# Value products of two steps of four scores issued together in three groups of a turn

## What is computed

```python
...
    x = _L0_conv_ref(x, ...)   # group norm, attention over channels (32x32 per head), projection, + x
    x = _L1_conv_ref(x, ...)   # one head, 32 channels, softmax over 1024 positions, value of 128 channels
    x = _L2_conv_ref(x, ...)   # group norm, 8 heads of 32 channels, softmax over 1024 positions, projection, + x
    x = _L3_conv_ref(x, ...)   # the same with other weights, and the normed image added at the end
...
        sim = jnp.einsum('bhdi,bhdj->bhij', q, k)
        attn = jax.nn.softmax(sim, axis=-1)
        out = jnp.einsum('bhij,bhdj->bhid', attn, v)
```

## Time and profile before

| what | value |
|---|---|
| median of three runs | 3087.99 us |
| the profiled execution | 3084.11 us |
| its span, first to last instruction | 3082.3 us |
| mean granted TensorE clock | 0.963 |
| PE (TensorE matmul) busy | 2846.6 us, 92% |
| POOL (GpSimd) busy | 2179.4 us, 71% |
| DVE (VectorE) busy | 1858.1 us, 60% |
| ACT (ScalarE) busy | 1553.3 us, 50% |
| PE's share of the chain that ended last | 64% |

### The profile page before, as it was taken

How to read it: one execution, slowest core, us unless ns; L and a number is a source line. 1 busy time by engine, 2 the same in 40 slices (tenths; PEclk the granted TensorE clock), 3 DMA queues, 4 the chain that set the end, 5 groups by cost and what they waited for, 6 DMA issues and landing times.

```text
span 3082.3 us, 36214 instructions
## 1 busy us (share of the span) xinstructions
PE 2846.6 (92%) x13152; PEld 1405.6 (46%) x13152; DVE 1858.1 (60%) x3293; ACT 1553.3 (50%) x2794; POOL 2179.4 (71%) x746
## 2 busy tenths in 40 slices
PE   6688979999999999999999999999999999999998
PEld 4345434544445444554445544464444544444442
DVE  1264557557665667556675666756766576767663
ACT  1233435445564455545554555644555445555554
POOL 3225757677775877768776777867777587798877
PEclk8779989999999999999999999999999999999999
DMA  2240054133341234330343323503343123333340
GB/s 72 44 67 13 23 80 68 24 43 56 44 83 24 32 57 71 57 53 16 43 87 40 53 45 48 90 14 43 57 64 62 30 39 43 57 56 43 43 58 15
DMA packets 74388, 150.87 MB, mean 49 GB/s; under 512 B 9121, under 2 KB 10657, under 8 KB 74210
## 3 DMA queue, kind: packets, MB, share of 16 engines
q1 hardware_dynamic: 74210, 148.56, 31.9%
HBM read 20.46 MB, written 16.78 MB: 12 GB/s over the span
## 4 chain that ended last, share of the span: by engine, by line
PE 64%; DMA 12%; ACT 9%; DVE 8%; issue 3%; POOL 3%; SPq 2%; ACTq 0%; POOLq 0%; DVEq 0%
PE psum L1277 15%; PE psum L1302 11%; PE psum L1246 10%; DMA Q<-lo 7%; PE psum L1221 6%; PE psum L1190 5%; ACT prob L907 4%; PE psum L1198 4%; DVE maxpart L1030 3%; PE psum L1298 3%; DMA K<-hi 3%; PE psum L1123 2%; DMA Q<-max_rows 2%; DVE stats L939 2%; PE psum L1323 2%
## 5 line engine op out<-in xcount | busy, mean ns | idle before, releaser
L1030 DVE TENSOR_REDUCE maxpart<-psum 128x1 f32<-128x512 f32 x2176 | 1412.0, 684 | 816.5 <-PE psum L1246 793.0
L907 ACT ACTIVATE prob<-psum 128x512 f32<-128x512 f32 x2176 | 1226.3, 596 | 960.9 <-PE psum L1277 925.1
L803 POOL TENSOR_TENSOR acc<-acc,prob 128x2048 f32<-128x2048 f32 (+1 forms) x322 | 1151.9, 3577 | 178.8 <-ACT prob L907 150.4
L1277 PE MATMUL psum<-Q,K 104*128 104x512 f32 x2048 | 1081.1, 530 | 96.1 <-ACT prob L907 73.6
L1246 PE MATMUL psum<-K,Q 96*128 96x512 f32 x2048 | 837.9, 413 | 36.9 <-DMA K<-hi 20.5
L1277 PEld LDWEIGHTS psum<-Q,K 104*128 104x128 f32 x2048 | 391.3, 192 | 799.0 <-ACT prob L907 474.1
L1302 PE MATMUL psum<-prob,vT 128*32 128x512 f32 x4096 | 577.0, 623 | 0.0
L803 POOL TENSOR_TENSOR vT<-vT,prob 128x2048 f32<-128x2048 f32 x123 | 560.8, 4559 | 19.4 <-ACT prob L907 8.3
L1246 PEld LDWEIGHTS psum<-K,Q 96*128 96x128 f32 x2048 | 399.8, 195 | 188.9 <-issue 90.9
L803 POOL TENSOR_TENSOR acc<-prob 128x2048 f32<-128x2048 f32 (+1 forms) x58 | 212.0, 3655 | 385.8 <-PE psum L1323 210.2
L1302 PEld LDWEIGHTS psum<-prob,vT 128*32 128x32 f32 x4096 | 100.6, 110 | 200.8 <-ACT prob L907 114.3
(11 more groups left out here) (121 smaller groups left out, 2130.4 us busy)
## 6 DMA issues: line engine op xcount, KB each, us to landing
Q<-hi SPq DMA_DIRECT2D x128, 256.0 KB
K<-hi SPq DMA_DIRECT2D x128, 256.0 KB
Q<-lo SPq DMA_DIRECT2D x64, 256.0 KB
K<-lo SPq DMA_DIRECT2D x64, 256.0 KB
xa<-in_x SPq DMA_DIRECT2D x8, 1024.0 KB, 8.5
scratch<-xa SPq DMA_DIRECT2D x8, 1024.0 KB, 4.0
xb<-scratch SPq DMA_DIRECT2D x8, 1024.0 KB, 4.9
out<-hb SPq DMA_DIRECT2D x7, 1024.0 KB, 5.8
```

Source lines behind the costliest of these rows:

```text
L803: pool.tensor_tensor(total, first if a == 1 else total, this, ALU.add).then_inc(added, 1)
L907: act.activation(prob[STEP_STARTS.slot(b, start)][:, j, :], score_bank[(SCORES.rank[b.n][e] - 1) % SCORE_BANKS], ACT.Exp, scale=1.0 if lay ...
L1030: dve.tensor_reduce(maxpart[layer][:, a // NQ, a % NQ:a % NQ + 1], bank, AX_X, ALU.max).then_inc(max_free, 1)
L1277: pe.matmul(score_bank[(r - 1) % SCORE_BANKS], left, right, start=True, stop=True).then_inc(score_full, 1)
```

## The change

For the groups (2, 2), (2, 3) and (3, 0) of turns 3 to 8 (`PAIRED`), the list `late` is emptied only at the ends of the even steps. So the bundles of steps s - 2 and s - 1 are issued behind one another at the end of an even step s, and none at the end of an odd one. A `finish` that falls due in such a group waits in `pending` for the same place. `invert` and `scale` get their due times from where the finish was put, two and five slots behind it. The output pieces of layer 2 in (3, 0) of the steady turns start four slots later.

```diff
--- before.py
+++ after.py
@@ -38,6 +38,7 @@
 MAXIMA = {1: QT * NQ, 2: HPT * QT * NQ, 3: HPT * QT * NQ, LAST3: HPT * QT * NQ}
 
 LAG = HPT
+PAIRED = {(2, 2), (2, 3), (3, 0)}
 FINISH_AFTER = 4
 INVERT_AFTER = 6
 SCALE_AFTER = 9
@@ -186,7 +187,7 @@
     third = [(2, 0, [(0, ("reload",))] + spread(0, 14, late2) + spread(14, 18, late_halves) + spread(18, end, out2),
               [(2, 1, 0, 32, 0, 23), rows(2, 1, 27), (2, 2, 0, 8, 24, 31)])]
     steady = (layer2(True, True)
-              + [(3, 0, spread(0, 14, late3) + spread(SCALED, end, out2),
+              + [(3, 0, spread(0, 14, late3) + spread(SCALED + 4, end + 1, out2),
                   [(3, 1, 8, 16, 0, 7), (1, 0, 0, 8, 8, 15), rows(1, 0, 19), (1, 1, 0, 8, 16, 23), rows(1, 1, 27),
                    (3, 1, 16, 24, 24, 31)]),
                  (1, 0, [], [(3, 1, 24, 32, 0, 7)]),
@@ -241,18 +242,33 @@
         plan.append(x)
         if x[0] == "values" and x[3] == STEPS[x[1]] - 1:
             plan.append(("evacuate",) + x[1:3])
-            pending.extend((clock + after, (kind,) + x[1:3]) for kind, after in
-                           (("finish", FINISH_AFTER), ("invert", INVERT_AFTER), ("scale", SCALE_AFTER)))
+            pending.append((clock + FINISH_AFTER, ("finish",) + x[1:3]))
+
+    def finished(of, now):
+
+        for kind, after in (("invert", INVERT_AFTER), ("scale", SCALE_AFTER)):
+            pending.append((now + after - FINISH_AFTER, (kind,) + of))
+        pending.sort(key=lambda x: x[0])
 
     turns = group_sequence()
-    for groups in turns:
+    for n, groups in enumerate(turns):
         plan = []
         for at, (layer, g, pieces, maxima) in enumerate(groups):
             if layer is None:
                 while late:
+                    if late[0][0] == "value" and late[0][3:] == (0, 0):
+                        while pending:
+                            x = pending.pop(0)[1]
+                            plan.append(x)
+                            if x[0] == "finish":
+                                finished(x[1:], clock)
                     advance(plan)
-                plan += [x for _, x in pending] + flat(pieces if ("max", 2, 0, 0) in pieces else cut(pieces))
-                pending.clear()
+                while pending:
+                    x = pending.pop(0)[1]
+                    plan.append(x)
+                    if x[0] == "finish":
+                        finished(x[1:], clock)
+                plan += flat(pieces if ("max", 2, 0, 0) in pieces else cut(pieces))
                 if at + 1 < len(groups) and groups[at + 1][0] == 1:
                     to = groups[at + 1][:2]
                     plan += [("max",) + to + (a,) for a in range(MAXIMA[to[0]])] + [("split",) + to, ("maxrow",) + to]
@@ -261,6 +277,8 @@
             pieces = sorted(pieces, key=lambda x: x[0])
             for slot in range(slots):
                 s, j = slot // HPT, slot % HPT
+                paired = groups is turns[3] and (layer, g) in PAIRED
+                with_values = j == HPT - 1 and (s % 2 == 0 or not paired)
                 plan.append(("score", layer, g, s, j))
                 late.append(("values", layer, g, s) if j == HPT - 1 else ("value", layer, g, s, j))
                 turning = []
@@ -274,15 +292,17 @@
                                  for a in range(n * (slot - low) // of, n * (slot - low + 1) // of)]
                         if slot == high and stop == MAXIMA[to_layer]:
                             plan.append(("split", to_layer, to_g))
-                while pending and pending[0][0] <= clock:
+                while pending and pending[0][0] <= clock and (with_values or pending[0][1][0] != "finish"):
                     x = pending.pop(0)[1]
                     (turning if x[0] == "finish" else plan).append(x)
+                    if x[0] == "finish":
+                        finished(x[1:], clock)
                 while pieces and (pieces[0][0] <= slot or slot == slots - 1):
                     plan += flat([pieces.pop(0)[1]])
                 if turning:
                     close(plan, pieces)
                     plan += turning
-                while j == HPT - 1 and len(late) > LAG:
+                while with_values and len(late) > LAG:
                     advance(plan)
                 clock += 1
         for x in [x for x in plan if x[0] == "finish"]:
```

## The result

The changed kernel takes **3148.9 us** (median of 6 runs, 3130.01 to 3157.3), the kernel before in the same sessions 3090.49 us (6 runs). The ratio is **1.0184, 95% interval 1.0153 to 1.0216**: slower by 58 us. The forecast had the sign, with 0.60, but 3113 us; the result lies 18 us above the upper end of the range.

The account below looks back on a forecast made before the run. TensorE bounds (2, 2) and (2, 3), POOL's chain the end of (3, 0). Per turn -0.5 + 3.6 + 1.1 = +4.2 us, six turns +25 us on the 3087.99 us median: 3113 us, range 3082 to 3131.

Parts of the forecast that it names:

- the sign: Whole kernel: slower than before, at chance 0.60, with about 0.5% (15.4 us) as the limit for no change.
- Merge saves 0.32 us: TensorE: two bundles issued as one run save 0.32 us, 72 merges 23 us, where TensorE sets the end.
- The exponential, +0.7: Group (2, 2): without the finish as cover, TensorE waits 0.7 us for the exponential behind ACT's hi copy.
- The bank, +1.5: Group (2, 2): the second rows piece waits 1.5 us for side0_free, released by the first transpose of invert.
- The scale in (3, 0): POOL: the scale starts 5.1 us later, some 22 to 23 us into (3, 0) instead of 17.6.
- TensorE at the finish: Group (3, 0): TensorE reaches the finish by about 1037 and idles some 6 us until POOL's last add.
- POOL's chain: Group (3, 0): finish, invert, scale and six adds in one 28 us block set the end; forecast chance 0.55.
- +3.6 for the finish: Group (3, 0): the finish comes at 1043.2 against a mean of 1039.6 before, +3.6 us per turn.
- (2, 2) and (2, 3) within 1 us of 50.5 and 52.1: Both groups nearly even: waits +0.7 and +1.5, xa wait -0.5, seven merges -2.2, sum -0.5 us per turn.
- the clock term: Idle ahead of the finish of (3, 0) drops the clock: 1.6 us in two of three turns, +1.1 per turn.
- The tiling mode decides: Rival, faster: side work keeps ahead of TensorE and all 72 merges count, 3062 us; chance 0.11.
- ACT did not starve: Rival, slower: TensorE waits one more exponential (0.6 us) after each bundle pair, 43 us on top, 3133 us; chance 0.08.

Follow-up runs that it names:

- (2, 2) alone: The changed kernel with only the four merges of group (2, 2), its finish moved; (2, 3) and (3, 0) as before the change: 3127.15 us, ratio 1.0112.
- (2, 3) alone: The changed kernel with only the four merges of group (2, 3): 3073.35 us, ratio 0.9947 to the kernel before.
- (3, 0) alone: The changed kernel with only the four merges of (3, 0), its finish moved and output pieces four slots later: 3139.84 us, ratio 1.0166.
- first of (3, 0): The changed kernel with one merge per turn, steps 0 and 1 of (3, 0), finish of (2, 3) one step later: 3114.97 us, ratio 1.0071.
- first of (2, 2): The changed kernel with one merge per turn, steps 0 and 1 of (2, 2), finish of (2, 1) one step later: 3113.59 us, ratio 1.0064.
- scale late, twelve: The changed kernel, all twelve merges, with the scale of (2, 3) four slots later, behind adds 2 and 3: 3129.94 us, ratio 1.0115.
- finish kept, nine: The changed kernel with three merges per group, none of step 0 with 1, so no finish moves: 3087.52 us, ratio 0.9977.

## Why the prediction was right in sign and short in size

**Three terms are enough.** For the six turns of each traced kernel I take the change of TensorE's idle time, half the change of the time at half speed, and 0.32 us off per merge. Against the change of the turns' length, in us over six turns:

| kernel | idle | half of half speed | merges | sum | measured |
|---|---|---|---|---|---|
| changed, twelve | +22.9 | +63.1 | -23.0 | +63.0 | +61.3 |
| (2, 2) alone | +9.8 | +51.2 | -7.7 | +53.3 | +47.9 |
| (2, 3) alone | -10.0 | -3.4 | -7.7 | -21.0 | -21.8 |
| (3, 0) alone | +27.0 | +41.0 | -7.7 | +60.3 | +57.1 |
| first of (3, 0) | +11.2 | +20.5 | -1.9 | +29.8 | +29.9 |
| first of (2, 2) | +10.8 | +18.8 | -1.9 | +27.7 | +30.2 |
| scale late, twelve | +21.4 | +47.8 | -23.0 | +46.2 | +48.2 |
| finish kept, nine | -3.4 | +17.1 | -17.3 | -3.6 | -1.2 |

All fifteen kernels fit within 6 us. In the changed kernel the merges and the idle time cancel, and what is left is the clock. Of the 22.9 us of idle DVE ends 15.3 (the bank in (2, 2) is 8.5 of these), POOL 7.8, ACT 4.5; what DMAs end is 4.6 less.

**Merge saves 0.32 us: right**, by this table, and -2.3 us per turn with (2, 3) alone, where 4 x 0.32 + 0.5 = 1.8 was forecast.

**The exponential, +0.7: right in kind.** 0.38 to 0.58 us of idle. **The bank, +1.5: right as a wait** (1.41); the fall of the clock in two of six turns comes on top, 1.1 us per turn.

**The scale in (3, 0): right.** The forecast put it 22.7 us in, measured are 23.5 to 24.7. But it counted from 991.0 and at the same time let the bundle that stood before the group go, which starts the group 1.2 us earlier: in the group's own count it said 23.9 us for the scale and 53.4 us for the finish, and the mean finish is at 53.3. This trace's SP and ACT rows show the steps of the estimate:

```profile
1009.24 1.28 SPq L721 DMA_DIRECT2D Q<-hi  x2
```

```profile
1018.09 0.69 ACT L875 ACTIVATE hi<-psum,const_sb 128x512 fp32r<-128x512 f32 x1 [2.05 <-DMA Q<-lo]
...
1024.30 0.69 ACT L875 ACTIVATE hi<-psum,const_sb 128x512 fp32r<-128x512 f32 x1 [3.77 <-DMA Q<-lo]
```

```profile
1026.86 1.29 DVE L1050 TENSOR_REDUCE maxpart<-psum 128x1 f32<-128x512 f32 x2 [1.14 <-PE psum L1266]
```

8.85 us from issue to copy (taken: 9.07), 6.21 to the next (taken: 6.3), and the first stack issued 3.9 us into the group as before. Not foreseen is the DVE row: ahead of invert it waits 1.14 us for TensorE's maximum products. The six adds took 28.06 us (28.13).

**TensorE at the finish: wrong.** The forecast had it there by 1037, 47.2 us in by the same count, to wait 6 us. It was there at 52.0 and waited 1.3. It stood idle for 3.4 us in (3, 0) ahead of the finish where it was 1.5, and 20 us more at half speed over six turns are 1.7 us per turn. So the two chains are nearly even, and the time of the finish came out right although the late scale alone decides only the last 1.3 us of it (the run with the scale later: 1.6). The forecast's picture, POOL's chain with TensorE waiting far ahead of it, does not hold; that its +3.6 for the finish was met owes something to luck.

**(2, 2) and (2, 3) within 1 us of 50.5 and 52.1: wrong.** -0.5 per turn was forecast, +3.9 measured. The order is not what was mis-sized: 68 us more at half speed are 5.7 us per turn, and without them the two groups would stand at -1.8, which is the -0.5 less the bundle of 1.2 us that went over to (3, 0).

**The failed step is the clock term.** I charged one fall of 1.6 us in two of three turns, +1.1, behind the one long idle that I foresaw. The trace has 126 us more at half speed in six turns, up to 10 us of time per turn, and the forecast as a whole was short by 6 per turn (+4.2 against +10.2). Where the 126 us begin: some 55 at the border of (2, 2) and (2, 3), without any wait in front; 14 right behind the wait of 1.41 us in (2, 2), which I had only in my upper end; 24 in (3, 0) and (1, 0); 37 in (3, 1) and (2, 1), which the change doesn't touch; and 3 less in (3, 2). The falls at the border and in the untouched groups I had put at nothing, without a reason. Why the clock falls at the border is open. For (3, 1) at least it isn't the work on (3, 0): the kernel with (2, 3) alone, the fastest of all, has the same 246.9 us there, 37.5 at half speed.

**Rivals.** "The tiling mode decides" is what happens with (2, 3) alone. ACT did not starve: scores waited 0.38 to 0.58 us once per (2, 2) turn, not after each pair, and what ACT ends of the idle time grew by 4.5 us over six turns, where the rival wanted 43. It would have come near the measured time all the same (3133 us), for a reason that the trace does not show.

## What to carry to other kernels

Price a wait on TensorE at more than its length: here 1.4 us of it cost 2.6 us a turn on average with the falls of the clock right behind it. Ask what stands in front of a wait whose end something else sets: a bundle there was free, and taken away from there it came back behind the wait and cost its full length. Where an in-order engine carries both a late one-off (the scale) and a row of fixed work (six adds), count how many of the latter stand behind the former, and then ask whether the other engine would be there any earlier: here it would have been by 1.3 us. Keep an account by terms (idle, clock, work) over the same turns before and after; a group's window misleads when work crosses its border. And leave the steps alone at which something is released for others: of the sets tried, none gave more than the four merges of (2, 3).

## What the runs showed that was not expected

The granted clock fell under full load: behind 50 small products in 3.60 us without idle it was 0.50 for the next 7 us. The same instructions in the same order took 53.00 and 58.70 us in two turns of one execution, and the same wait of 1.41 us had a fall behind it in two turns of six. And the clock reached into places with no edit: (2, 2) and (2, 3), left as they were, had 0 to 31 us at half speed at their border in five kernels; with merges in (2, 3) alone (3, 1) had 37.5 us where it was 13.6; and in the changed kernel (2, 1), far behind the last merge, ran at 0.83 in its last turn (40.20 us where 37.10 to 38.40 were usual).
